# One-core graph and expert kernel: register loads grouped by batches, stores cut by 32 partitions, and half of a product on ScalarE

## The chip, the cores and the metric

The kernel runs as one program on 1 core of a Trainium2 chip. The metric is the device time of one launch in microseconds (us), the median of 3 runs. A profiled execution is a launch of its own; its span runs from the first to the last instruction of the program.

The engines are named as the profile does: PE is TensorE's matmul, PEld its weight load, DVE is VectorE, ACT is ScalarE, POOL is GpSimd, and SP is SyncE, which issues most DMAs. A letter q behind a name (SPq, PEldq, DVEq) marks an entry of that engine's sequencer, which waits, loads registers or issues DMAs.

## The reference

The input is 3125 nodes with 256 features, 50000 edges (src, dst, weight), and the weights of 16 experts. After a layer norm, three rounds of sparse times dense follow, each with an L2 normalisation of the rows, and the mean over the input and the rounds is added to x. Then come a second layer norm and a mixture of experts (2 of 16 for each node), with a layer norm behind it.

```python
def _spmm(vals, row, col, h, n_nodes):
    msgs = vals[:, None] * h[col]
    return jax.ops.segment_sum(msgs, row, num_segments=n_nodes, indices_are_sorted=True)
...
    for _ in range(LAYERS):            # 3
        h = _spmm(vals, row, col, h, n_nodes)
        h = _l2_normalize(h)
        acc = acc + h
    return acc / (LAYERS + 1)
...
    x = x + _L0_gnn_ref(_layernorm(x, axis=-1), edge_weight, src, dst)
    x = x + _L0_ffn_ref(_layernorm(x, axis=-1)[None], ...)[0]
```

The call gives `src` as `row` and `dst` as `col`, and the edges are sorted by `dst`.

## The kernel before

The kernel makes the sparse matrix dense once, and then does the three rounds as dense products. Its phases follow each other with a barrier between them: tables, build (0 to about 474 us of the profile together), rounds, route, experts, combine. The change is in the build phase, in one table it reads, and in the address from which the rounds load what it stored.

**The build phase.** The dense matrix has a row for each dst node and a column for each src node (3200 columns, as 20 groups HI of LO = 160). Six nodes (CW) make a window, so a window is M = 6 x 20 = 120 partitions by 160 columns. A step takes one tile of 128 edges, in the partitions, against one window: the matmul of a one-hot of (node in window, column group), weighted by the edge's value, with a one-hot of the column in its group gives the window's sum. The value is split into three bf16 parts, so each step has three matmuls. B = 12 steps make a batch, and there are NB = 76 batches; all 12 windows of a batch stand in four PSUM banks, three windows a bank.

For one batch b the engines do this:

- DVE: `key_hot` (128x1536, a comparison with `key_tab`), `lo_hot` (128x1920), and three products `key_w[k] = key_hot * part k` (function `weigh`, 128x1536 each). Then `carry` of batch b-2: the window in which batch b-3 ended may go on in batch b-2, and its sum is added to the first window (128x160). For this DVE needs a register with the place of that window, which `slot_of` loads at the start of each run.
- PE: waits until batch b-2 is out of PSUM, loads 12 registers with the PSUM places of the 12 steps (one TENSOR_LOAD of 12 words, line 513), opens the four banks with matmuls of 2 columns (line 518), waits for `hot_ready`, and issues 36 matmuls of 128x160 (line 523), with a register operation for each three.
- ACT: four copies PSUM to SBUF of 128x480 (`evacuate`, line 432) into `win`, a ring of RING = 4 batches. It waits for the stores of batch b-4, whose place it takes.
- SP: loads the number of the batch's first window (line 400), waits for `carried`, and stores 5 pieces of 24 partitions (line 406), one into each of 5 DRAM tensors `a_0` to `a_4`. Windows of consecutive batches overlap by design (the later store of a window is the full one), so each piece waits until the same piece of the batch before has landed.

The order of the work is written out by hand. `batches` writes four batches before a loop, four in the loop's body, and four behind it. The one-hots have two buffers, so DVE starts batch b only when PE has finished batch b-2.

**The rounds phase** loads, for each of 5 passes, blocks of 128 rows by 640 columns (2560 bytes a row) of the stored matrix (line 608), splits them in two parts on ACT and DVE, and multiplies. Each pass before has its own DRAM tensor, which is why the partitions of a window are ordered by pass in `key_tab` (five iotas of 48 elements, line 188).

## Time and profile before

| | us |
|---|---|
| runs | 1612.67, 1612.77, 1617.57; median 1612.77 |
| the profiled execution's own time | 1628.98 |
| its span | 1627.2 |
| build phase: first `key_hot` of DVE to first DMA of the rounds | 52.9 to 473.9 |

Over the span PE is busy 77% (1260.5 us), DVE 72%, ACT 45%, POOL 12%. These shares are means over phases with different limits; those of the build phase are among the rows below, in a table by stretch whose columns are the stretch, its length, then for PE, PEld, DVE, ACT and POOL the busy time with the number of instructions, then the granted TensorE clock as a share, the mean busy share of 16 DMA engines, and GB/s.

### The profile page before, as it was taken

To read this page: it belongs to the slowest core of one execution; us is meant where nothing else is said; L and a number is where in the kernel's file an instruction comes from. 1 tells how busy PE (TensorE), PEld (TensorE's weight loads), DVE (VectorE), ACT (ScalarE), POOL (GpSimd) and SP (SyncE) were. 2 spreads that over 40 slices of the span, in tenths; PEclk is the share of its full clock that TensorE was granted. 3 is DMA by queue.
4 is the path that set the end of the run, shared out by engine and by line. 5 is a ranking of instruction groups with operands and counts; after the bars stand their busy time and mean duration, and the time that the engine had idled before them with its cause. 6 is when DMAs were issued, how large, how long until landed. Compare 5 with 4: busy or idle time off the path is not lost. (4 is left out here: it accounts for less than half of the span.)

```text
span 1627.2 us, 30449 instructions
## 1 busy us (share of the span) xinstructions
PE 1260.5 (77%) x9152; PEld 1129.8 (69%) x9153; DVE 1173.7 (72%) x2074; ACT 730.1 (45%) x1401; POOL 196.1 (12%) x203
## 2 busy tenths in 40 slices
PE   4467667667738999999999999999574899999200
PEld 1456666666637888888888888888472899999200
DVE  8899999999927665765556756666555788988347
ACT  2333333333325555655554655555231666666102
POOL 1200000000000000000000000000250433332470
PEclk8798888888869999999999999999755899999655
DMA  2176677767677666666666656665140785344652
GB/s 94 48 177 173 173 179 180 179 173 182 178 213 217 186 186 185 184 174 186 183 186 178 194 168 185 185 184 181 45 157 30 233 277 184 101 111 94 194 162 72
DMA packets 229026, 267.32 MB, mean 164 GB/s; under 512 B 16061, under 2 KB 172356, under 8 KB 228960
## 3 DMA queue, kind: packets, MB, share of 16 engines
q1 hardware_dynamic: 205696, 234.01, 50.2%
q0 software_dynamic: 6624, 16.90, 3.8%
q10 hardware_dynamic: 16640, 15.73, 3.4%
q14 instruction: 50, 0.41, 0.1%
q8 instruction: 16, 0.26, 0.1%
HBM read 175.51 MB, written 91.07 MB: 164 GB/s over the span
## 5 line engine op out<-in xcount | busy, mean ns | idle before, releaser
L830 PE MATMUL ps_rows<-h_both,a_high 128*128 (+1 forms) x1875 | 506.6, 398 | 37.2 <-DVE a_low L710 31.9
L710 DVE TENSOR_TENSOR a_low<-a_raw,a_high 128x640 fp32r<-128x640 f32 x375 | 305.5, 823 | 236.2 <-ACT a_high L640 233.5
L640 ACT ACTIVATE a_high<-a_raw 128x640 fp32r<-128x640 f32 x375 | 274.4, 740 | 294.5 <-PE ps_rows L833 271.7
L830 PEld LDWEIGHTS ps_rows<-h_both,a_high 128*128 128x128 f32 x1875 | 330.8, 191 | 95.0 <-issue 32.3
L523 PE MATMUL ps_w<-lo_hot,key_w 128*128 128x160 bf16 x2736 | 257.6, 262 | 58.2 <-DVE key_w L459 57.6
L833 PEld LDWEIGHTS ps_rows<-h_both,a_low 128*128 128x128 f32 x1875 | 276.1, 191 | 32.9
L523 PEld LDWEIGHTS ps_w<-lo_hot,key_w 128*128 128x128 bf16 x2736 | 242.0, 111 | 64.4 <-issue 62.9
L833 PE MATMUL ps_rows<-h_both,a_low 128*128 (+1 forms) x1875 | 284.7, 283 | 0.0
L432 ACT ACTIVATE win<-ps_w 128x480 f32<-128x480 f32 x304 | 148.9, 576 | 261.1 <-DMA a<-win 156.0
L459 DVE TENSOR_TENSOR key_w<-key_hot,tab_marks 128x1536 bf16<-128x1536 bf16 x228 | 208.7, 949 | 0.0
L1318 POOL DMA_INDIRECT x_t<-tokens,r_token x80 | 92.6, 1157 | 141.5 <-PE ps_x L1445 128.7
L1390 DVE TENSOR_TENSOR w_low<-w_raw,w_high 128x1024 fp32r<-128x1024 f32 x80 | 94.4, 1220 | 20.7 <-ACT w_high L1332 14.0
L1332 ACT ACTIVATE w_high<-w_raw 128x1024 fp32r x80 | 80.4, 1052 | 60.9 <-PE ps_o L1477 47.8
L1460 PE MATMUL ps_h<-x_high,w_high 128*128 128x256 f32 x320 | 94.4, 295 | 0.0
L1460 PE MATMUL ps_h<-x_high,w_low 128*128 128x256 f32 x320 | 91.1, 285 | 0.0
L1460 PE MATMUL ps_h<-x_low,w_high 128*128 128x256 f32 x320 | 91.1, 285 | 0.0
L1477 PE MATMUL ps_o<-w_high,hid_high 128*128 128x256 f32 x320 | 90.0, 281 | 1.3 <-DVE hid_low L1405 1.3
L451 DVE TENSOR_TENSOR key_hot<-key_tab,tab_marks 128x1536 bf16<-128x1536 bf16 x76 | 72.7, 957 | 25.1 <-issue 17.4
L1477 PE MATMUL ps_o<-w_low,hid_high 128*128 128x256 f32 x320 | 90.0, 281 | 0.0
L1477 PE MATMUL ps_o<-w_high,hid_low 128*128 128x256 f32 x320 | 89.7, 280 | 0.0
L453 DVE TENSOR_TENSOR lo_hot<-lo_tab,tab_marks 128x1920 bf16<-128x1920 bf16 x76 | 87.4, 1150 | 0.0
L976 POOL MEMSET all_ones<- 128x800 f32 x1 | 0.8, 764 | 696.8 <-POOLq L537 696.8
(223 smaller groups left out, 1396.8 us busy)
## 6 DMA issues: line engine op xcount, KB each, us to landing
a_raw<-a SPq DMA_DIRECT2D x375, 320.0 KB, 3.1
a<-win SPq DMA_DIRECT2D x380, 180.0 KB
w_raw<-in_L_ffn_w SPq DMA_DIRECT2D x32, 512.0 KB
results_sorted<-y_t ACTq DMA_DIRECT2D x40, 256.0 KB
b_t<-in_L_ffn_b ACTq DMA_DIRECT2D x40, 128.0 KB
hf<-in_x SPq DMA_DIRECT2D x1, 3072.0 KB
x<-in_x SPq DMA_DIRECT2D x1, 3072.0 KB
tokens<-hf SPq DMA_DIRECT2D x4, 768.0 KB
```

What stands on the lines that cost most here:

```text
L432: ins = nc.scalar.activation(win[:, i, bank * WIDE:(bank + 1) * WIDE], ps_w[:, i % 2, bank * 512:bank * 512 + WIDE], ACT.Copy)
L453: v.tensor_tensor(lo_hot[:, u, :, :, :], tab.lo_tab[:].unsqueeze(1).broadcast_to([P, PAIRS, LO, 2]), mark(b, 1, LO), ALU.is_equal).then_in ...
L459: v.tensor_tensor(key_w[:, u, k, :, :, :], key_hot[:, u, :, :, :], mark(b, 2 + k, P), ALU.mult).then_inc(hot_ready, 1)
L523: ins = mm(ps_w[:, u, bass.DynSlice(places[j], LO)], key_w[:, u, k, j // 2, :, j % 2], lo_hot[:, u, j // 2, :, j % 2], start=False, stop=F ...
L640: a.activation(a_high[:, u, :], a_raw[:, u, :], ACT.Copy).then_inc(high_split, 1)
L710: v.tensor_tensor(a_low[:, u, :], a_raw[:, u, :], a_high[:, u, :].bitcast(F32), ALU.subtract).then_inc(low_split, 1)
L830: nc.tensor.matmul(ps[:, banks[w][r], :], a_high[:, u, r * P:(r + 1) * P], both, start=first, stop=False, skip_group_check=True)
L833: ins = nc.tensor.matmul(ps[:, banks[w][r], 0:D], a_low[:, u, r * P:(r + 1) * P], upper, start=False, stop=last, skip_group_check=True)
L1318: g.indirect_dma_start(out=x_t[:, t % 2, h, :], out_offset=None, in_=y_dram, in_offset=bass.IndirectOffsetOnAxis(ap=routes.token[:, t * HA ...
L1390: v.tensor_tensor(w_low[n][:, u, :], of_expert(w_raw[n], e), w_high[n][:, u, :].bitcast(F32), ALU.subtract).then_inc(w_low_ready[n], 1)
L1460: ins = mm(ps_h[:, u, f, :], w[0][:, u, at], x[:, u, k, :], start=(n == 0), stop=(n == 3 * KD - 1))
L1477: ins = mm(ps_o[:, u, half, :], h[:, u, f, tokens], w[1][:, u, at], start=(n == 0), stop=(n == 3 * KF - 1))
```

## The change

Four things change, all for the build phase.

1. **DVE's carry places.** `slots_of` loads the places of four batches in one register load at the head of the loop's body, where each batch had its own load. DVE's loop runs over 18 bodies of four batches, with four batches ahead of it.
2. **PE's places.** `multiply` loads 24 registers on even batches (two batches' places), and none on odd ones.
3. **Stores.** There is one DRAM tensor `a_rows` with all 120 partitions of a window in a row, and four stores of 32, 32, 32 and 24 partitions. `key_tab` is one iota in natural order, and the rounds load 2560 bytes out of each row of 12800. `zeros`, the source of the rows that no window covers, grows from 640 to 3200 columns, and five padding DMAs become one.
4. **Half of the third product on ScalarE.** DVE makes `key_w[2]` for 3 of 6 pairs of steps (128x768 in place of 128x1536). ACT makes the other 6 steps with one ACTIVATE of 128x128 each, with the weights as scale, after a copy of 12 weights into `third_b`. ACT does this for batch b ahead of the evacuation of batch b-1. DVE (before `key_hot`) and PE (before the matmuls) wait for it by `third_ready`.

```diff
-        zeros = sb("zeros", [P, s.GROUP * P])
+        zeros = sb("zeros", [P, s.HI * LO])
+        third_b = sb("third_b", [P, 2, B])
...
+        PARTS = [slice(p, min(p + 32, M)) for p in range(0, M, 32)]
...
-                for w in range(s.PASSES):
-                    part = slice(w * CW * s.HG, (w + 1) * CW * s.HG)
+                for n, part in enumerate(PARTS):
                     if late(b, 1):
-                        sp.wait_ge(stored[w], b * 16)
-                    sp.dma_start(a_dram[w][bass.DynSlice(base, B), :, :].rearrange("i p l -> p i l"),
-                                 win[part, i, :].rearrange("p (i l) -> p i l", l=LO)).then_inc(stored[w], 16)
+                        sp.wait_ge(stored[n], b * 16)
+                    sp.dma_start(a_dram[bass.DynSlice(base, B), part, :].rearrange("i p l -> p i l"),
+                                 win[part, i, :].rearrange("p (i l) -> p i l", l=LO)).then_inc(stored[n], 16)
...
+            def third(b, u):
+
+                if late(b, 2):
+                    act.wait_ge(multiplied, b - 1)
+                    act.wait_ge(third_ready, (b - 1) * BY_ACT)
+                nc.scalar.activation(third_b[:, u, :], tab.marks[:, 4, steps(b)], ACT.Copy).then_inc(third_read, 1)
+                act.wait_ge(third_read, b + 1)
+                act.wait_ge(key_ready, b + 1)
+                for j in range(2 * DVE_PAIRS, B):
+                    nc.scalar.activation(key_w[:, u, 2, j // 2, :, j % 2], key_hot[:, u, j // 2, :, j % 2], ACT.Copy,
+                                         scale=third_b[:, u, j:j + 1]).then_inc(third_ready, 1)
...
-            batches(act, evacuate)
+            def run(b, i):
+                third(b, i % 2)
+                if late(b, 1):
+                    evacuate(b - 1, (i - 1) % RING)
...
+                n = DVE_PAIRS if k == 2 else PAIRS
                 dve.wait_ge(key_ready, b + 1)
-                v.tensor_tensor(key_w[:, u, k, :, :, :], key_hot[:, u, :, :, :], mark(b, 2 + k, P),
+                v.tensor_tensor(key_w[:, u, k, 0:n, :, :], key_hot[:, u, 0:n, :, :], mark(b, 2 + k, P)[:, 0:n, :, :],
                                 ALU.mult).then_inc(hot_ready, 1)
...
+            with dve.Fori(1, NB // RING) as it:
+                slots = slots_of(it * RING - 2, RING)
+                for i in range(RING):
+                    run(it * RING + i, i, slots[i])
...
                 if late(b, 2):
                     pe.wait_ge(evacuated, b - 1)
-                _, places = nc.values_load_multi_w_load_instructions(
-                    tab.place[0:1, steps(b)], engines=[mybir.EngineType.PE], min_val=0,
+                if u == 0:
+                    both = slice(b * B, (b + 2) * B) if isinstance(b, int) else bass.DynSlice(b * B, 2 * B)
+                    places[:] = nc.values_load_multi_w_load_instructions(
+                        tab.place[0:1, both], engines=[mybir.EngineType.PE], min_val=0,
...
                 pe.wait_ge(hot_ready, (b + 1) * 4)
+                pe.wait_ge(third_ready, (b + 1) * BY_ACT)
```

**PE, from the end of one batch to the end of the next but one, in the loop.** `tab_place` is the table of places, `ps_w` the PSUM banks, "ISA" a register operation. Before, every batch has its load:

```order
L523 MATMUL ps_w<-lo_hot,key_w 128x160 x3
L513 ISA [waits evacuated]
L513 TENSOR_LOAD tab_place
L518 MATMUL ps_w<-none 128x2 x4
L520 ISA
L523 ISA [waits hot_ready_b]
```

Now the even batch (the first six rows) has a load, and the odd one (the last six) has none:

```order
L547 ISA [waits evacuated]
L547 TENSOR_LOAD tab_place
L552 MATMUL ps_w<-none 128x2 x4
L554 ISA
L555 REGISTER_ALU [waits hot_ready_b]
L558 ISA [waits third_ready]
...
L552 MATMUL ps_w<-none 128x2 [waits evacuated]
L552 MATMUL ps_w<-none 128x2 x3
L554 ISA
L555 REGISTER_ALU [waits hot_ready_b]
L558 ISA [waits third_ready]
L558 MATMUL ps_w<-lo_hot,key_w 128x160 x3
```

It is still one load instruction, of twice the words, and it keeps its place ahead of the even batch's matmuls.

**ACT, one batch in the loop.** `win` is the ring that the stores read, `third_b` the copied weights. Before, a batch is its evacuation alone:

```order
L426 REGISTER_ALU
L428 REGISTER_ALU [waits carried]
L430 REGISTER_ALU [waits stored_3,stored_4,stored_2,tabs,stored_1,stored_0]
L432 ACTIVATE win<-ps_w 128x480 [waits multiplied]
L432 ACTIVATE win<-ps_w 128x480 x3
```

Now seven small operations of the next batch stand ahead of it:

```order
L429 ACTIVATE third_b<-tab_marks 128x12
L430 REGISTER_ALU
L433 ACTIVATE key_w<-key_hot,third_b 128x128 [waits key_hot_ready,third_read]
L433 ACTIVATE key_w<-key_hot,third_b 128x128 x5
L438 REGISTER_ALU
L440 REGISTER_ALU [waits carried]
L444 ACTIVATE win<-ps_w 128x480 [waits stored_3,tabs,stored_2,multiplied,stored_1,stored_0]
L444 ACTIVATE win<-ps_w 128x480 x3
```

The evacuation of batch b-1 is queued behind the small operations of batch b, which wait for DVE's `key_hot` of batch b.

## Rows read from the trace of the kernel before

**Rows 1.** The page: the span, busy time, and busy share of the DMA engines in 40 slices

```profile
span 1627.2 us, 30449 instructions
PE 1260.5 (77%) x9152; PEld 1129.8 (69%) x9153; DVE 1173.7 (72%) x2074; ACT 730.1 (45%) x1401; POOL 196.1 (12%) x203
DMA  2176677767677666666666656665140785344652
```

**Rows 2.** Busy time of each engine in the batch stage and in what follows it

```profile
75.00:455.00 380.00, 262.21 (x2876) 244.76 (x2876) 355.84 (x504) 142.35 (x292) 0.00 (x0) 0.85 0.69 176
455.00:475.00 20.00, 0.00 (x0) 0.00 (x0) 0.81 (x2) 0.59 (x2) 0.31 (x1) 0.51 0.63 160
```

**Rows 3.** The page: groups of instructions, with one duration and the idle time before

```profile
L432 ACT ACTIVATE win<-ps_w 128x480 f32<-128x480 f32 x304 | 148.9, 576 | 261.1 <-DMA a<-win 156.0
L459 DVE TENSOR_TENSOR key_w<-key_hot,tab_marks 128x1536 bf16<-128x1536 bf16 x228 | 208.7, 949 | 0.0
L453 DVE TENSOR_TENSOR lo_hot<-lo_tab,tab_marks 128x1920 bf16<-128x1920 bf16 x76 | 87.4, 1150 | 0.0
```

**Rows 4.** Two lines of VectorE: durations, and the first and last start

```profile
L451 DVE TENSOR_TENSOR key_hot<-key_tab,tab_marks x76: 946/958/960, 52.9 to 444.0; 128x1536 bf16<-128x1536 bf16 x76
L479 DVE SCALAR_TENSOR_TENSOR win<-win,same_b x76: 372/376/385, 66.6 to 455.3; 128x160 f32<-128x160 f32 x76
```

**Rows 5.** Timeline from 370 to 383 us: start, length, and idle time before

```profile
371.87 2.75 PE L523 MATMUL ps_w<-lo_hot,key_w 128*128 128x160 bf16 x36 [0.17 <-DVE key_w L459]
375.69 0.24 PE L518 MATMUL ps_w<-none 128*128 128x2 bf16 x4 [1.07 <-issue]
376.85 4.33 PE L523 MATMUL ps_w<-lo_hot,key_w 128*128 128x160 bf16 x36 [0.93 <-DVE key_w L459]
376.92 0.96 DVE L451 TENSOR_TENSOR key_hot<-key_tab,tab_marks 128x1536 bf16<-128x1536 bf16 x1
377.79 1.15 DVE L453 TENSOR_TENSOR lo_hot<-lo_tab,tab_marks 128x1920 bf16<-128x1920 bf16 x1
378.86 1.82 DVE L459 TENSOR_TENSOR key_w<-key_hot,tab_marks 128x1536 bf16<-128x1536 bf16 x2
381.53 0.38 DVE L479 SCALAR_TENSOR_TENSOR win<-win,same_b 128x160 f32<-128x160 f32 x1
381.83 0.95 DVE L451 TENSOR_TENSOR key_hot<-key_tab,tab_marks 128x1536 bf16<-128x1536 bf16 x1
```

**Rows 6.** Register loads: all of L513, those before 74 us, one alone, and L469

```profile
L513 PEldq TENSOR_LOAD <-tab_place x76: 855/2286/3171, 52.9 to 445.0; - x76
L513 PEldq TENSOR_LOAD <-tab_place x5: 855/1054/1669, 52.9 to 73.5; - x5
L513 PEldq TENSOR_LOAD <-tab_place x1: 2338/2338/2338, 373.3 to 373.3; - x1
L469 DVEq TENSOR_LOAD <-tab_slot x76: 302/506/1407, 58.4 to 449.3; - x76
```

**Rows 7.** TensorE in two stretches, each of one batch, with the granted clock

```profile
252.85:256.00 3.15, 2.76 (x37) 1.00 0.71 180
257.79:262.05 4.26, 4.23 (x36) 0.62 0.71 176
```

**Rows 8.** The stores of line 406, and the first DMAs after them

```profile
L406 SPq DMA_DIRECT2D a<-win x380: 302/762/1682, 75.2 to 469.4; - x190
473.89 2.28 SPq L608 DMA_DIRECT2D a_raw<-a  x5
```

**Rows 9.** Timeline: two memsets of GpSimd; and groups of small operations on ScalarE

```profile
50.56 0.63 POOL L419 MEMSET zeros<- 128x640 f32 x1
51.13 1.70 POOL L420 MEMSET win<- 128x1920 f32 x1
...
L646 ACT ACTIVATE h_both<-hf 128x256 fp32r<-128x256 f32 x75 | 29.7, 401 | 18.8 <-DVEq L800 18.8
L1344 ACT ACTIVATE b_t<-r_b 128x4 f32 x34 | 6.6, 194 | 0.0
```

More of the change, by code:

```diff
@@ L185, in _ @@
             g.memset(ones[:], 1.0).then_inc(iotas, 1)
[L186 to L189 removed]
+            g.iota(tab.key_tab[:, 0:M, :], pattern=[[1, M], [0, 2]], base=0, channel_multiplier=0, **kw)
             g.memset(tab.key_tab[:, M:P, :], -2.0)
@@ L360, in phase_build @@
         same_read = sem("same_read")
+        third_read = sem("third_read")
+        third_ready = sem("third_ready")
         key_ready = sem("key_hot_ready")
@@ L366, in phase_build @@
         padded = sem("padded")
-        stored = [sem(f"stored_{w}") for w in range(s.PASSES)]
+        PARTS = [slice(p, min(p + 32, M)) for p in range(0, M, 32)]
+        stored = [sem(f"stored_{n}") for n in range(len(PARTS))]
         block = ctx.enter_context(nc.Block())
@@ L381, in batches @@
         def batches(eng, run):
-            for i in range(RING):
-                run(i, i)
-            with eng.Fori(1, NB // RING - 1) as it:
+            for b in range(2 * RING):
+                run(b, b % RING)
+            with eng.Fori(2, NB // RING - 1) as it:
                 for i in range(RING):
@@ L394, in _ @@
             sp.wait_ge(tabs, 3)
-            for w in range(s.PASSES):
-                rows = a_dram[w].rearrange("i (c n) l -> (i c) (n l)", c=CW)[first:s.CH * P, :]
-                sp.dma_start(rows, zeros[0:s.CH * P - first, :]).then_inc(padded, 16)
+            sp.dma_start(a_dram.rearrange("i (c n) l -> (i c) (n l)", c=CW)[first:s.CH * P, :],
+                         zeros[0:s.CH * P - first, :]).then_inc(padded, 16)
             def store(b, i):
@@ L426, in evacuate @@
                     act.wait_ge(carried, b - 2)
-                    for w in range(s.PASSES):
-                        act.wait_ge(stored[w], (b - 3) * 16)
+                    for done in stored:
+                        act.wait_ge(done, (b - 3) * 16)
                 act.wait_ge(tabs, 3)
@@ L434, in evacuate @@
                 ins.then_inc(evacuated, 1)
-            batches(act, evacuate)
+            def run(b, i):
+                third(b, i % 2)
+                if late(b, 1):
+                    evacuate(b - 1, (i - 1) % RING)
+            batches(act, run)
+            evacuate(NB - 1, (NB - 1) % RING)
         @block.vector
@@ L466, in same, with slots_of @@
                 v.tensor_copy(same_b[:, u:u + 1], tab.same[:, one(b)]).then_inc(same_read, 1)
-            def slot_of(b):
-                return dve.value_load(tab.slot[0:1, one(b)], min_val=0, max_val=(B - 1) * LO)
+            def slots_of(b, n):
+                at = slice(b, b + n) if isinstance(b, int) else bass.DynSlice(b, n)
+                _, values = nc.values_load_multi_w_load_instructions(
+                    tab.slot[0:1, at], engines=[mybir.EngineType.DVE], min_val=0, max_val=(B - 1) * LO,
+                    skip_runtime_bounds_check_because="a slot is LO times the minimum with B - 1 of a count")
+                return values
             def carry(b, i, slot):
@@ L480, in carry, with run @@
                                        win[:, i, start], ALU.mult, ALU.add).then_inc(carried, 1)
-            def run(b, i):
+            def run(b, i, slot):
                 u = i % 2
-                slot = slot_of(b - 2) if late(b, 2) else None
                 one_hots(b, u)
@@ L494, in _ @@
             dve.wait_ge(tabs, 3)
-            batches(dve, run)
+            slots = slots_of(0, 2)
+            for b in range(RING):
+                run(b, b, slots[b - 2] if b >= 2 else None)
+            with dve.Fori(1, NB // RING) as it:
+                slots = slots_of(it * RING - 2, RING)
+                for i in range(RING):
+                    run(it * RING + i, i, slots[i])
+            slots = slots_of(NB - 2, 2)
             for b in (NB - 2, NB - 1):
-                slot = slot_of(b)
                 same(b, b % 2)
-                carry(b, b % RING, slot)
+                carry(b, b % RING, slots[b - (NB - 2)])
         @block.tensor
@@ L507, in _ @@
                    start=True, stop=True, skip_group_check=True)
+            places = []
             def multiply(b, i):
@@ L1665, in program @@
     s = Sizes(x.shape[0], x.shape[1], src.shape[0], gate_w.shape[1], w1.shape[2])
-    a_dram = [nc.dram_tensor(f"a_{w}", [s.WALL, s.CW * s.HG, s.LO], F32, kind="Internal").ap()
-              for w in range(s.PASSES)]
+    a_dram = nc.dram_tensor("a_rows", [s.WALL, s.M, s.LO], F32, kind="Internal").ap()
     y_dram = nc.dram_tensor("tokens", [s.N, s.D], F32, kind="Internal").ap()
```

24 lines of the change are left out of this document (11 added, 13 removed).

## The prediction, written before the changed kernel ran

> **What bounds the kernel now.** I start with the page: the span is 1627.2 us and no engine is busy all through, so the answer has to come by phase [rows 1]. The table by stretch shows the phase that the change touches, 75 to 455 us: VectorE is busy 355.84 of 380 us, TensorE 262.21, ScalarE 142.35, and the DMA engines 0.69 of their time, a share that stays between 6 and 7 tenths in every slice of the phase [rows 1, 2]. VectorE's own two lines give the pace. `key_hot` starts at 52.9 us for batch 0 and at 444.0 for batch 75, so a batch takes (444.0 - 52.9) / 75 = 5.21 us [rows 4]. In the timeline one batch goes from 376.92 to 381.83 without idle time: 4.91 us [rows 5]. The other 0.30 us are the mean of what the register load of the carry place leaves uncovered (`tab_slot`, 302 to 1407 ns, [rows 6]). So VectorE sets the phase, and it is not alone.
>
> Two others are near. TensorE needs 2.75 us for its 36 matmuls where the granted clock is 1.00 (2.4 GHz), and 4.2 to 4.3 where the stretch's mean is 0.62, most of it at 1.2 GHz [rows 5, 7]; between two batches it has an idle stretch that the page puts down to "issue", which is its own register load: in the timeline matmuls end at 374.62, the load that began at 373.3 takes 2.34 us to 375.63, and the bank openers follow at 375.69 [rows 5, 6]. The stores are the other: ScalarE's evacuation waits 156.0 us for them in all [rows 3], the last carry starts at 455.3 and the last store is issued at 469.4, 14 us later, and the rounds' first DMA at 473.89 [rows 4, 8]. A store queue that ends that late had no room to catch up.
>
> **VectorE's part.** From 1536 to 1920 elements the operation grows from 949 to 1150 ns [rows 3], 0.523 ns an element. Half of `key_w[2]` is 768 elements less: 0.40 us off each batch, 4.91 to 4.51. Of the place loads one in four stays, with four words. Its price lies between nothing (covered as most of the one-word loads are) and four times the dearest, 5.6 us a load; I take about 0.45 us uncovered, near what the one-word median of 506 ns with some words more gives, so 0.11 a batch. VectorE alone would then run at 4.62 us a batch.
>
> **ScalarE's part.** Evacuations cost 148.9 / 76 = 1.96 us a batch [rows 3]. A 128x128 operation lies between 194 ns (128x4) and 401 ns (128x256) [rows 9]; I take 0.29. Six and the copy of 12 weights (0.19) are 1.9 us, at most 2.6. Sum 3.9, at most 4.6 us: it fits under 5 us, but just about under 4.62. The order also fits: `third(b)` can begin 0.96 us after `key_hot(b)` starts and is done at about 2.9; TensorE's batch b-1 begins at that same start (376.85 and 376.92) and ends 2.75 to 4.33 us later [rows 5]. So the evacuation queued behind `third` is late by nothing in most batches, and `third_ready` comes 1.5 us ahead of VectorE's last product, for which TensorE waits anyway. Cost: nothing; if the operations cost 0.40 each, 0.1 to 0.2 us a batch in the case where VectorE bounds.
>
> **TensorE's part, which decides.** The change halves the number of place loads but doubles the words of each. A load of 12 words took 1.05 us (median) before the stores begin, at 74 us, and 2.29 us over all 76, at most 3.17 [rows 6]. So it is paid by the word, and the more so the busier the DMAs are. The least load of 12 words took 0.855 and the least load of one word 0.302 us, though on another engine: about 0.05 a word and 0.25 fixed. A load of 24 is twice the 12 less one fixed part: 2 x 2.29 - 0.25 = 4.3 us under today's traffic, 2 x 1.05 - 0.25 = 1.9 us without stores; the outer ends are 1.5 and 6.3 us. The traffic falls, as four stores take the place of five and the same bytes go out in less queue time, so I go a fifth of the way from 4.3 to 1.9: 3.8 us.
>
> What covers it is the sequencer's lead: the load began 1.3 us before the last matmul ended [rows 5, 6]. That lead doesn't grow with the words. From the end of the load to the first matmul another 0.35 us pass (375.63, the openers' 0.24, and the step to the matmuls). Two batches then take: idle 3.8 - 1.3 + 0.35 = 2.85; 36 matmuls after that pause, at the lower clock for most of them, 4.25 (as 4.23 and 4.33 after pauses in rows 5 and 7); openers 0.3; 36 matmuls after a busy stretch, 2.75. Sum 10.15, or 5.08 us a batch, in general load + 6.35 for two. That is above VectorE's 4.62: the bound moves to TensorE, and nearly all of VectorE's saving turns into a wait before `key_hot` for `multiplied`. The gain of the phase is (5.21 - 5.08) x 75 = 10 us.
>
> The Trainium skill (Runtime: NRT & Kernel Launch, section Instruction fetch mechanics) has a rule that speaks against this edit: such a load costs about 200 ns a register, even in bulk. The trace has 191 ns a word in the median of the loads under traffic and 88 before it, so it agrees only with stores in flight. By the page 24 words would take 4.8 us, which as an estimate gives 11.15 us for two batches.
>
> **The stores.** The same bytes leave in four pieces. SP issued 380 stores between 75.2 and 469.4 us, one in 1.04 us, without catching up. If time goes by the piece (24 or 32 partitions alike) a batch's stores fall from 5.2 to 4.2 us; if by the bytes, they stay at 5.2. I take 4.2 to 4.5, as the share of 0.69 leaves DMA engines unused. Then the queue catches up within the phase, and the end gains: today 473.9 - 455.3 = 18.6 us from the last carry to the rounds. Afterwards three more issues of 1.04, the 4.5 us from the last issue to the rounds as now [rows 8], and about 0.9 for carry and base load: 8.5. Gain 10 us.
>
> The Trainium skill (DMA: Bandwidth & Descriptors, section Why a DMA increments its semaphore by 16 and not by 1) says that a DMA runs on the largest number of engines up to 16 that divides the outer sizes: 12 for 24 partitions, 16 for 32. The busy share of 0.69 fits under the 0.75 that 12 of 16 allow. By it the busiest engines would carry 8/10 of the rows, the 4.2 us above; without it the 5.2 of the rival below.
>
> **The start.** VectorE waits for the memset of `win`, which stands behind `zeros` (0.63 us for 640 columns, 1.70 for 1920, [rows 9]). At 0.83 ns a column 3200 columns cost 2.1 us more, and the whole phase begins that much later. The iotas of `key_tab` run long before it, and the padding moves the same bytes. The rounds read the same 2560-byte rows with another step; TensorE bounds there, and I cost that at nothing.
>
> **Sum**, against the profiled execution's own 1628.98: -10 (phase) -10 (end) +2 (start) = -18, so 1611. The runs' median lies 16 us below that execution; the same difference from 1612.8 gives 1594 us.
>
> **Rivals.**
> - The load is cheap. If 24 words take under 2.9 us, two batches of TensorE fall under 2 x 4.62, and VectorE bounds at 4.62. For it: five loads of 12 words took 1.05. Against: the median of all 76, most of them under traffic, is more than twice that. The time: (5.21 - 4.62) x 75 = 44, with end and start 52 us less: 1561.
> - The load is dear, and the kernel gets slower. The place is the pause of TensorE ahead of each even batch. It eats the other 8 us from 4.3 us a load on (two batches in 10.65); at 4.8 us it is 5.58 a batch, 27 us more in the phase, and with end and start 1632. For it: 2 x 2.29, and the dearest 12 words (3.17); against: fewer stores in flight. The page's 200 ns a register would put it here.
> - The stores keep their 5.2 us a batch, as bytes and rows are the same. Then ScalarE's evacuation holds everything to the old pace, and the end doesn't shrink: +2, 1615, or a few us less or more by how the load falls. For it: the 156 us that ScalarE waits for them.
>
> **Chances.** The forecast 0.50, cheap load 0.16, dear load 0.22, stores 0.12. The forecast's own range is 1578 to 1611, for loads of 3.4 to 4.3 us. I take 0.3% (5 us) as what a measurement of this kernel can tell from no change. Faster: 0.43 of the forecast's 0.50, and 0.16, together 0.59. Within 0.3%: 0.07 of the forecast and 0.07 of the stores, 0.14. Slower: 0.22 and 0.05, 0.27. For 8 in 10 the range reaches from the cheap load's 1562 to the dear load's 1632.
>
> **What would show it.** The loads of `tab_place` in the new trace: 38, with a median near 3.8 us. The wait of `key_hot` should be put to PE and no longer to issue; the even batches of TensorE slow, the odd ones at 2.75 us. `key_w` of 768 elements at about 547 ns. ScalarE busy near 3.9 us a batch, hardly waiting for stores. The last store within 5 us of the last carry. VectorE's first `key_hot` at about 55 us. I am wrong in the mechanism if VectorE stays without waits, or if ScalarE waits for `a_rows` as long as now; and in the size if the median load lies outside 3.4 to 4.3 us.

## The result, and the profile after

The changed kernel takes 1605.12 us (median of 6 runs, 1603.68 to 1606.47) against 1612.72 us for the kernel before beside it (6 runs, 1611.52 to 1618.16). The ratio is 0.9948, 95% interval 0.9934 to 0.9961: faster by half a per cent. The forecast was 1594 us (18 less), with a range of 1562 to 1632. The direction and the range hold; the gain is less than half of what was forecast.

The page of the changed kernel, the lines that answer to [rows 1], and its table by stretch, which answers to [rows 2]; the second columns are the time that a stretch lasts, then each engine's busy time, the mean granted clock, the DMA share and GB/s:

```profile
span 1604.1 us, 31106 instructions
PE 1259.8 (79%) x9152; PEld 1135.5 (71%) x9153; DVE 1137.9 (71%) x2074; ACT 875.4 (55%) x1933; POOL 209.8 (13%) x199
DMA  3187777677787666656666666666222587334373
```
```profile
75.00:455.00 380.00, 257.39 (x2881) 246.85 (x2880) 325.47 (x507) 279.80 (x794) 0.00 (x0) 0.83 0.75 180
```

VectorE lost work (355.84 to 325.47 us of 380), ScalarE doubled its own (142.35 to 279.80), and the DMA share rose from 0.69 to 0.75. The two profiled spans differ by 23 us, yet the medians by 7.6: the execution of before that was profiled ran long by 16 us, so the spans must not be subtracted. The phases up to the end of the rounds can be: from there to the end of the program the profile before takes 468.1 us and the changed one 450.8, and that is where the excess lies.

The lines of VectorE that answer to [rows 4], the register loads that answer to [rows 6], and the first transfer of the rounds, as in [rows 8] (a load's line gives least, median and longest ns, then first and last start):

```profile
L470 DVE TENSOR_TENSOR key_hot<-key_tab,tab_marks x76: 944/949/959, 55.1 to 443.4; 128x1536 bf16<-128x1536 bf16 x76
L504 DVE SCALAR_TENSOR_TENSOR win<-win,same_b x76: 371/376/385, 67.6 to 453.3; 128x160 f32<-128x160 f32 x76
```
```profile
L491 DVEq TENSOR_LOAD <-tab_slot x20: 782/2286/3541, 54.3 to 447.6; - x20
L547 PEldq TENSOR_LOAD <-tab_place x38: 1622/3310/4654, 54.3 to 440.3; - x38
```
```profile
465.27 0.85 SPq L643 DMA_DIRECT2D a_raw<-a_rows  x2
```

From these the 8.6 us by which the rounds start earlier (473.89 to 465.27) add up: the start is 2.2 later (52.9 to 55.1), the 75 batches take 388.3 in place of 391.1 (2.8 less, pace 5.18 after 5.21), the step from the last `key_hot` to the last carry 1.4 less, and from there to the rounds 12.0 in place of 18.6 us, 6.6 less. So the end gave most of what it should; the phase, which should have given 10 us, gave 3. At the end SyncE was still late: its last load of a base starts 3.1 us after the last carry has ended (453.7), and the last store is issued at 460.4.

```profile
L401 SPq TENSOR_LOAD <-tab_base x76: 467/728/1170, 74.3 to 456.8; - x76
```

What ate the phase stands in the timeline, from one batch (381.61) to the two after it. Start, length, what, and in brackets the idle time before it:

```profile
381.32 0.38 DVE L504 SCALAR_TENSOR_TENSOR win<-win,same_b 128x160 f32<-128x160 f32 x1
381.61 0.95 DVE L470 TENSOR_TENSOR key_hot<-key_tab,tab_marks 128x1536 bf16<-128x1536 bf16 x1
383.31 0.24 PE L552 MATMUL ps_w<-none 128*128 128x2 bf16 x4 [3.46 <-issue]
383.63 4.98 PE L558 MATMUL ps_w<-lo_hot,key_w 128*128 128x160 bf16 x36
385.82 0.38 DVE L504 SCALAR_TENSOR_TENSOR win<-win,same_b 128x160 f32<-128x160 f32 x1
388.55 3.19 PE L558 MATMUL ps_w<-lo_hot,key_w 128*128 128x160 bf16 x36
389.37 0.96 DVE L470 TENSOR_TENSOR key_hot<-key_tab,tab_marks 128x1536 bf16<-128x1536 bf16 x1 [3.18 <-PE ps_w L558]
```
```profile
L491 DVEq TENSOR_LOAD <-tab_slot x1: 2923/2923/2923, 386.1 to 386.1; - x1
```

One batch passes in 4.50 us (381.32 to 385.82), as VectorE alone would have it. Then VectorE stands still for 3.18 us. The view blames TensorE, whose matmuls ended at 388.61; but the four-word load that began at 386.1 ended only at 389.0, and `key_hot` starts 0.3 us behind that. The two limits end 0.4 us apart, and either alone would hold the batch. The new waits in the build phase (75 to 450 us, total, times, longest):

```profile
PE ps_w L552 <- issue: 90.9, 36, 4.2
ACT win L444 <- PE ps_w L558: 57.6, 23, 3.9
DVE key_hot L470 <- PE ps_w L558: 31.2, 14, 3.8
DVE key_hot L470 <- issue: 17.3, 7, 3.1
ACT win L444 <- DMA a_rows<-win: 12.9, 8, 4.4
```

The stores are out of the way (156.0 us of ScalarE's waiting became 12.9). `key_hot` now waits for both TensorE and its own load. Within each four batches, the first three pass at about 4.5 us and the one that ends in VectorE's load at 7.3 (means over batches 8 to 74, from the starts of `key_hot`: 4.51, 4.63, 4.50, 7.33).

### The profile page after: what moved, and what is told of

It is laid out like the page before. It is cut to its first block and busy times, and to the rows that moved or that the text cites. A ratio compares the mean times of both kernels' runs of the same rounds, so it can differ in the third digit from the quotient of the medians.

```text
span 1604.1 us, 31106 instructions
## 1 busy us (share of the span) xinstructions
PE 1259.8 (79%) x9152; PEld 1135.5 (71%) x9153; DVE 1137.9 (71%) x2074; ACT 875.4 (55%) x1933; POOL 209.8 (13%) x199
## 5 line engine op out<-in xcount | busy, mean ns | idle before, releaser
L479 DVE TENSOR_TENSOR key_w<-key_hot,tab_marks 128x1536 bf16<-128x1536 bf16 (+1 forms) x228 | 178.2, 814 | 0.0
L433 ACT ACTIVATE key_w<-key_hot,third_b 128x128 bf16<-128x128 bf16 x456 | 144.5, 426 | 38.2 <-DVE key_hot L470 36.9
L1353 POOL DMA_INDIRECT x_t<-tokens,r_token x80 | 104.4, 1305 | 131.5 <-PE ps_x L1480 118.7
L1425 DVE TENSOR_TENSOR w_low<-w_raw,w_high 128x1024 fp32r<-128x1024 f32 x80 | 94.4, 1220 | 17.6 <-ACT w_high L1367 12.9
L552 PE MATMUL ps_w<-none 128*128 128x2 bf16 x304 | 18.9, 166 | 91.3 <-issue 91.3
```

The source lines that it names most:

```text
L433: nc.scalar.activation(key_w[:, u, 2, j // 2, :, j % 2], key_hot[:, u, j // 2, :, j % 2], ACT.Copy, scale=third_b[:, u, j:j + 1]).then_inc ...
L479: v.tensor_tensor(key_w[:, u, k, 0:n, :, :], key_hot[:, u, 0:n, :, :], mark(b, 2 + k, P)[:, 0:n, :, :], ALU.mult).then_inc(hot_ready, 1)
L1353: g.indirect_dma_start(out=x_t[:, t % 2, h, :], out_offset=None, in_=y_dram, in_offset=bass.IndirectOffsetOnAxis(ap=routes.token[:, t * HA ...
L1425: v.tensor_tensor(w_low[n][:, u, :], of_expert(w_raw[n], e), w_high[n][:, u, :].bitcast(F32), ALU.subtract).then_inc(w_low_ready[n], 1)
```

## The experiments

The theory T: VectorE's four-word load, uncovered at the head of the loop body, and TensorE's pair of batches with its 24-word load are two limits nearly level. Taking away one runs into the other. The rivals: R1, VectorE's load is the only limit; R2, TensorE's load is, as the prediction had it. The times are medians of 5 to 12 executions beside the kernel before, unless said otherwise. Each kernel has one profile, and that one execution can lie some us off the median. What the profiles show of the phases:

| | pace, us a batch | first DMA of the rounds | rounds, first to last start of a matmul |
|---|---|---|---|
| before | 5.21 | 473.9 | 680.5 |
| changed | 5.18 | 465.3 | 683.3 |
| `a_covered` | 5.05 | 453.6 | 683.2 |
| `a_slots1` | 5.20 | 464.5 | 680.3 |
| `a_places12` | 5.25 | 469.7 | 680.1 |
| `a_both1` | 5.14 | 460.3 | 680.2 |
| `b_stores` | 5.43 | 482.7 | 680.2 |
| `b_half` | 5.28 | 478.8 | 681.3 |
| `c_cov12_row127` | 4.90 | 454.1 | 683.5 |
| `c_cov12` | 4.70 | 428.9 | 680.5 |
| `c_best` | 4.63 | 426.3 | 679.6 |

No edit touches the rounds; what the 3 us there are is told where the prediction is answered.

**VectorE's load covered (`a_covered`).** The same load, moved behind the second product of the body's first batch:

```diff
                 weigh(b, u, 1)
+                if load is not None:
+                    slots[:] = slots_of(load, RING)
...
-                slots = slots_of(it * RING - 2, RING)
```

> Changed kernel, but VectorE's load of four carry places stands behind the second weighed product of the body's first batch, where the sequencer would otherwise wait, and no longer at the loop head ahead of key_hot. Theory T (two limits nearly level: VectorE's four-word load at the loop head, 2.29 us in the median and 2.8 us of pause per four batches; TensorE's 24-word load): the pause ahead of key_hot goes, TensorE's load stays, a batch takes 5.0 to 5.1 us where it took 5.21, so 8 to 15 us less than the changed kernel, 1590 to 1597. Rival R1 (VectorE's load is the only limit, TensorE's pause is slack): 4.55 to 4.65 a batch, 1560 to 1566. Rival R2 (TensorE's load alone sets the pace, VectorE's load lies in its shadow): no change, 1605, and key_hot waits for PE by 2.8 us in four batches.

Measured 1592.16 us (1586.66 to 1595.88), ratio 0.9858 [0.9836, 0.988]: 13 us under the changed kernel, with nothing of the work removed. One such load and the operations on either side of it, and the waits of the phase:

```profile
L491 DVEq TENSOR_LOAD <-tab_slot x1: 3327/3327/3327, 358.0 to 358.0; - x1
```
```profile
358.54 1.82 DVE L479 TENSOR_TENSOR key_w<-key_hot,tab_marks 128x1536 bf16<-128x1536 bf16 x2
361.49 0.15 DVE L486 COPY same_b<-tab_same 128x1 f32 x1 [1.13 <-issue]
```
```profile
DVE key_hot L470 <- PE ps_w L564: 25.5, 20, 2.5
DVE same_b L486 <- issue: 10.2, 14, 1.5
```

The load takes 3.33 us, longer than where it stood, and yet costs 1.13, because two products were already queued when it began. What is left is TensorE (25.5 us in 20 waits). R1 (1560 to 1566) and R2 (1605) fall, T stands. The pace of 5.05 us is what the prediction had for TensorE alone (5.08).

**One-word loads on VectorE (`a_slots1`)**, each at the head of the batch that carries, instead of four words:

```diff
-                slots = slots_of(it * RING - 2, RING)
                 for i in range(RING):
-                    run(it * RING + i, i, slots[i])
+                    run(it * RING + i, i, slots_of(it * RING + i - 2, 1)[0])
```

> Changed kernel, but VectorE loads one carry place at the head of each batch, as before the change. T: each one-word load (0.5 us) leaves 0.2 to 0.3 us uncovered, VectorE alone would run at 4.8, TensorE's 24-word load holds the pace at 5.0 to 5.1: 1590 to 1599. R1: 4.75 to 4.85 a batch, 1575 to 1580. R2: 1605.

Measured 1601.31 us (1600.63 to 1602.83), 0.9923 [0.9906, 0.9941]: 4 us under the changed kernel, 2 above the upper end of T's range. But the build phase hardly moved. Its pace is 5.20 us where T had 5.0 to 5.1, the rounds start 0.8 us earlier than in the changed kernel, and 3.0 us of the difference between the two profiles lie in the rounds. TensorE fills this pace by itself: its load of 24 words takes 3.60 us here (mean of batches 8 to 71) and starts 0.69 us before the matmuls ahead of it end; with 0.37 us on to the next matmuls, 3.99 and 2.88 us for two batches of them and 0.30 between, a pair makes 10.5 us. T had the right limit and too low a price. The one-word load took 695 ns, not the 506 of before.

**Twelve words on TensorE (`a_places12`)**, loaded for every batch, VectorE's four-word load left:

```diff
-                if u == 0:
...
-                        tab.place[0:1, both], engines=[mybir.EngineType.PE], min_val=0,
+                    tab.place[0:1, steps(b)], engines=[mybir.EngineType.PE], min_val=0,
```

> Changed kernel, but TensorE loads 12 places for each batch, as before the change; VectorE's four-word load stays at the loop head. T: VectorE's 4 x 4.5 + 2.8 us for four batches stay, 5.2 a batch, so 1603 to 1606. R1: the same, 1605. R2 (TensorE's 24-word load alone): a pair of batches falls from 10.4 to about 9.9, and the time by 10 to 20 us, 1585 to 1595.

Measured 1606.59 us (1602.93 to 1608.64), 0.9952 [0.9934, 0.9969], the changed kernel's time within the scatter and half a us above T's range. With VectorE's load in the way TensorE's grouping doesn't show in the time. In the profiles the rounds start 4.4 us later than in the changed kernel and are 3.2 us shorter, so a small gain of the grouping is not excluded.

**Neither grouping (`a_both1`)** (both edits above; the stores and ScalarE's half product stay):

> Changed kernel without both groupings of loads: new stores and the half product on ScalarE alone. T: VectorE 4.8 a batch, TensorE with 12 words each near 4.9 to 5.0: 1585 to 1595, under each of the kernels that undo one grouping. R1: 4.8 a batch, 1575 to 1580, the same as with the single carry places alone. R2: as with the 12 places alone, 1585 to 1595.

Measured 1600.39 us (1598.41 to 1602.76), 0.9918 [0.99, 0.9935], 5 us under the changed kernel, but 5 above T's range. So the two grouped loads as they were placed cost more than they saved (in the profiles the rounds start 5.0 us earlier). T had the price of the ungrouped loads too low; `b_stores` shows why.

**The stores alone (`b_stores`)**, added to the kernel before (its a_rows buffer and four stores a batch, three of 32 partitions and one of 24; the text below says three):

> The kernel before with the changed a_rows buffer, iota and stores alone (three stores of whole rows by 32 partitions); the loads of places and VectorE's third product stay as before. Theory T (in the middle of the build phase VectorE's own chain and TensorE's pace, not the stores, set the pace): the pace stays within 0.05 of before's 5.215 us a batch, the tail from the last carry to the rounds' first a_raw transfer falls from 18.6 us to about 11, the start costs about 2 us; time 1604 to 1609 us, ratio about 0.996. Rival (the stores set before's pace: ScalarE waited 156 us for them): the pace falls by 0.1 us or more a batch as well, 1590 to 1600 us. Rival (the whole rows cost nothing and bring nothing): 1613 us.

Measured 1620.38 us (1615.0 to 1624.74, 11 runs), 1.0045 [1.003, 1.0059]: slower, against every theory. Its lines of VectorE, and waits in the phase:

```profile
L446 DVE TENSOR_TENSOR key_hot<-key_tab,tab_marks x76: 946/958/960, 54.3 to 461.4; 128x1536 bf16<-128x1536 bf16 x76
L464 DVEq TENSOR_LOAD <-tab_slot x76: 307/890/1097, 59.8 to 467.5; - x76
```
```profile
DVE key_hot L446 <- issue: 32.5, 62, 1.0
ACT win L427 <- DMA a_rows<-win: 9.5, 2, 4.9
```

The first of these waits in the kernel before, in the same stretch:

```profile
DVE key_hot L451 <- issue: 17.2, 37, 1.0
```

The stores no longer hold ScalarE, and the end is shorter (from the last `key_hot` to the rounds 21.3 us in place of 29.9). But the pace went from 5.21 to 5.43. In the kernel before, SyncE issued a batch's stores 6.4 us (mean) behind its carry; now they go out 0.16 us (median) behind it, upon VectorE's next load, whose median rises from 506 to 890 ns. VectorE has no slack there, so the 0.2 us a batch is paid in full: its waits for its own load grow by 15.3 us (17.2 to 32.5), and the 75 batches by 16. A faster store queue made another engine slower.

**Half the third product alone (`b_half`)**, the kernel before with that edit:

> The kernel before with half of the third product moved to ScalarE alone; stores and register loads as before. If VectorE's own work sets before's pace, it falls by up to the 0.40 us a batch that the half product takes, and the time would be 1583 to 1590 us. If the stores of before (about 5.2 us from issue to landing) or TensorE's pair of batches are level with VectorE, as T says, the pace falls by no more than 0.1 us a batch and the time is 1605 to 1613 us; a_both1 (both edits, 1600.4 us, pace 5.140) then holds about the sum of this and b_stores.

Measured 1616.09 us (1613.58 to 1625.29, 12 runs), 1.0023 [1.0008, 1.0039]: slightly slower, and above both ranges. (The 5.2 us in the text is the time in which a batch's stores leave; no run shows it as one store's way from issue to landing.)

```profile
ACT win L449 <- DMA a<-win: 62.0, 50, 3.7
ACT key_w L438 <- DVE key_hot L475: 30.2, 31, 1.6
DVE key_hot L475 <- issue: 25.2, 36, 1.6
DVE key_hot L475 <- ACT key_w L438: 23.5, 32, 1.7
```

With the old stores ScalarE's queue has an evacuation that waits for a store ahead of the next half product, and VectorE waits for ScalarE in turn (SyncE is 8.8 us behind the carries here, mean). Each part alone costs 3 to 7 us; both together (`a_both1`) gain 13. Neither could be priced alone; that they remove each other's bound is how I read it: without the old stores ScalarE's wait for them is 18.2 us in `a_both1` and not 62.0.

**What makes a load dear (`a_row127`).** The first idea, theory P, was the memory side of partition 0, which the first stores read too. Tables on all partitions, loads from row 127 (SyncE's is shown, the other two are changed alike):

```diff
-                base = sp.value_load(tab.base[0:1, one(b)], min_val=0, max_val=s.W - 1)
+                base = sp.value_load(tab.base[127:128, one(b)], min_val=0, max_val=s.W - 1)
```

> The changed kernel, with the tables of slots, places and bases worked out on all 128 partitions and the register loads of VectorE, TensorE and SyncE reading row 127 instead of row 0. Theory P (the loads are dear because the stores read the carried rows of the same partitions' side of the memory at the same moment; two of three stores touch the lower 64 partitions): VectorE's four-word load falls from 2.29 us to about 1.0 to 1.5, TensorE's 24 words from 3.31 to about 2.3 to 2.8, pace 4.8 to 5.0, 1575 to 1595 us. Rival (any store under way slows a load, whichever partition it reads): loads within 0.2 us of the changed kernel's, time 1603 to 1608 us. Rival (no relation to stores): the same, 1605 us; the two rivals are told apart by loads that start while no store is under way.

Measured 1605.08 us (1602.7 to 1606.74), 0.9945 [0.9929, 0.9961], no change. VectorE's loads take 2149 ns in the median, TensorE's 3706, SyncE's 1076 (2286, 3310 and 728 in the changed kernel): nothing gained, that idea is wrong.

**Thin stores (`a_thin`, `b_thin`).** Each store cut to one partition, so that its data is 1/24 to 1/32; the rest of the output rows is filled with zeros ahead of the first store, which lengthens the start. One profile each, read from 200 to 400 us only:

```diff
-                                 win[part, i, :]
+                                 win[part.start:part.start + 1, i, :]
```

> The changed kernel with each of its four stores a batch cut to one partition (the rest of the output rows is filled with zeros by transfers ahead of the first store, so the output differs and the start is longer; only the pace of the build phase is read). Theory S (VectorE's and TensorE's register loads are dear because store data moves at the same time): the four-word load falls from 2.29 us to about 1.0 and the 24-word load from 3.31 to about 1.65, as in the first batches, where no store is under way; the last batch of four falls from 7.33 to about 6.0 us and the pace from 5.18 to about 4.85 us a batch. Rival N (the loads are dear for a reason of their own, such as where they stand in the instruction stream): loads and pace within 5% of the changed kernel's.

> b_stores (the kernel before with the changed stores alone, pace 5.429, one-word load 0.89 us, twelve-word load 2.42) with each store cut to one partition, as in a_thin. Theory S: the one-word load falls to about 0.31 us, the twelve-word load to about 1.1, and since VectorE's chain sets the pace there, it falls by about the load's 0.58 us, to 4.85 to 4.95 us a batch. Rival N: pace within 0.1 us of 5.43. If the loads fall but the pace doesn't, VectorE's load was not on the path.

First the changed kernel with thin stores, then the `b_stores` kernel with them:

```profile
L492 DVEq TENSOR_LOAD <-tab_slot x10: 961/966/967, 208.4 to 392.1; - x10
L548 PEldq TENSOR_LOAD <-tab_place x20: 1717/1748/1757, 202.8 to 396.6; - x20
L407 SPq DMA_DIRECT2D a_rows<-win x157: 764/768/822, 200.6 to 399.3; - x157
L471 DVE TENSOR_TENSOR key_hot<-key_tab,tab_marks x40: 949/957/960, 199.1 to 397.9; 128x1536 bf16<-128x1536 bf16 x40
```
```profile
L465 DVEq TENSOR_LOAD <-tab_slot x39: 300/326/369, 202.5 to 396.6; - x39
L509 PEldq TENSOR_LOAD <-tab_place x39: 943/974/985, 202.4 to 396.2; - x39
L447 DVE TENSOR_TENSOR key_hot<-key_tab,tab_marks x39: 950/958/960, 203.3 to 397.4; 128x1536 bf16<-128x1536 bf16 x39
```

The DMA share in that stretch is 0.03. The four-word load falls from 2.29 to 0.97 us, 24 words from 3.31 to 1.75, one word from 0.89 to 0.33, 12 words from 2.42 to 0.97, and their spread all but vanishes. Store traffic in flight multiplies the price of a register load by 1.9 (24 words) to 2.7 (one word): theory S holds and N falls, on the loads. Bytes and packets fell together here, so which of the two it is stays open. On the pace it can't be read: both kernels run at 5.10 us a batch ((397.9 - 199.1) / 39; (397.4 - 203.3) / 38), because one-partition stores take SyncE 0.77 us each to issue. SyncE runs 12 us behind the carries and needs 5.0 us from the start of a base load to the end of the fourth issue, so it became the bound, and the expected 4.85 to 4.95 was missed.

**Both limits taken away (`c_cov12_row127`, `c_cov12`).** VectorE's load covered and 12 words on TensorE, reading row 127 and then row 0. The load stands behind the second product, as in `a_covered`; the first text says the first:

> The changed kernel with three edits: VectorE's four-word load moved behind the first product of the body's first batch (as in a_covered, 1592.2 us), twelve words of places per batch on TensorE (as in a_places12), and the register loads reading row 127 (as in a_row127). Theory T with P: pace 4.6 to 4.9 us a batch, 1560 to 1580 us. T alone (row 127 brings nothing): TensorE's pair with two loads of twelve words sets the pace at about 5.1 to 5.2, 1592 to 1600 us, no better than a_covered.

> c_cov12_row127 (1588.2 us, pace 4.897, held by the stores) with the register loads reading row 0 again, as the changed kernel does. SyncE's load of a base then takes about 0.8 us in place of 1.27. Theory: with both load costs out of the way, what is left is the last store's round trip (4.36 us from issue to landing, plus some 0.5 to the next issue), whichever row is read: pace 4.85 to 4.95, 1585 to 1592 us. If reading row 127 was what made the difference to a_covered, the pace goes back to 5.0 to 5.05 and the time to 1590 to 1596.

Row 127 took 1588.19 us (1587.72 to 1595.8), 0.9847 [0.983, 0.9865]. Row 0 took 1571.83 us (1566.57 to 1575.26), 0.9742 [0.9724, 0.9761], far below what was expected. T's own 5.1 to 5.2 us a batch for two loads of 12 words, and with it 1592 to 1600 us, was too slow for both.

With `c_cov12` the four combinations of the two loads are complete, and they are the proof of T:

| us | 24 words on TensorE | 12 words on TensorE |
|---|---|---|
| VectorE's load at the loop's head | 1605.12 (changed) | 1606.59 (`a_places12`) |
| VectorE's load covered | 1592.16 (`a_covered`) | 1571.83 (`c_cov12`) |

TensorE's 24 words cost 20 us once VectorE's load is covered, and nothing that shows while it isn't. The place of VectorE's load costs 13 us beside 24 words and 35 beside 12.

Why row 127 is the slower of the two shows in the trace. First row 127, then row 0, three views each: SyncE's base load, ScalarE's wait for the stores (75 to 420 us, and 75 to 405), and the row by engine of the same stretch:

```profile
L401 SPq TENSOR_LOAD <-tab_base x76: 478/1320/1411, 74.3 to 445.4; - x76
```
```profile
ACT win L444 <- DMA a_rows<-win: 68.6, 67, 2.2
```
```profile
75.00:420.00 345.00, 246.97 (x2788) 228.23 (x2786) 320.61 (x491) 273.50 (x764) 0.00 (x0) 0.87 0.80 186
```
```profile
L401 SPq TENSOR_LOAD <-tab_base x76: 463/890/1249, 74.2 to 420.5; - x76
```
```profile
ACT win L444 <- DMA a_rows<-win: 10.5, 11, 2.2
```
```profile
75.00:405.00 330.00, 222.96 (x2795) 205.37 (x2793) 318.50 (x490) 269.65 (x770) 0.00 (x0) 0.95 0.83 199
```

The pace is 4.90 against 4.70 us. My reason, the last store's own round trip of 4.9 us, is wrong, since the same stores with the same 2.7 to 4.4 us to landing went at 4.70. What differs is SyncE's base load, which stands between two batches' stores (1.32 against 0.89 us): SyncE is 9.3 us behind the carries with row 127 and 3.0 with row 0 (means), and ScalarE's wait follows it (68.6 against 10.5 us). The mean granted clock rose too, from 0.87 to 0.95. How the 0.2 us divides between the two I did not separate. The two profiled executions lie 29 us apart where the medians lie 16 apart, so these rows overstate the difference.

**The best version (`c_best`).** One-word loads on VectorE, each behind the second product of its batch; 12 words on TensorE, loaded before the wait for the evacuated buffer; `zeros` filled last, and only SyncE waits for it. The lines below are of the last two; VectorE's load stands behind the second product here too, not the first as the text says:

```diff
+            g.memset(win[:, RING - 1, :], 0.0).then_inc(tabs, 1)
             g.memset(zeros[:], 0.0).then_inc(tabs, 1)
-            g.memset(win[:, RING - 1, :], 0.0).then_inc(tabs, 1)
...
-            dve.wait_ge(tabs, 3)
+            dve.wait_ge(tabs, 2)
...
+                places[:] = nc.values_load_multi_w_load_instructions(
+                    tab.place[0:1, steps(b)], engines=[mybir.EngineType.PE], min_val=0,
...
                 if late(b, 2):
                     pe.wait_ge(evacuated, b - 1)
```

> The changed kernel with one-word place loads on VectorE, each behind the first product of its batch, twelve-word loads on TensorE moved ahead of the wait for the evacuated buffer, and the zeros for the end of the rows filled last, waited for by SyncE alone. VectorE's own work is about 4.5 us a batch plus at most 0.1 of load, TensorE's pair loses up to 0.7 us, the start loses the 2.2 us; the last store's round trip of 4.9 us is then the bound: pace 4.85 to 4.95, 1583 to 1590 us. If the loads don't stay covered, pace 5.05 to 5.15 and 1596 to 1604.

Measured 1561.47 us (1559.21 to 1567.9), 0.9679 [0.9656, 0.9702]: 44 us under the changed kernel, and 22 below the range's lower end, again because the stores' limit was set too high.

```profile
L470 DVE TENSOR_TENSOR key_hot<-key_tab,tab_marks x76: 949/956/960, 51.5 to 399.1; 128x1536 bf16<-128x1536 bf16 x76
L491 DVEq TENSOR_LOAD <-tab_slot x75: 300/672/1371, 60.8 to 403.3; - x75
```
```profile
ACT win L444 <- DMA a_rows<-win: 44.7, 63, 5.9
```

The pace is (399.1 - 51.5) / 75 = 4.63 us, the 4.51 of VectorE's own work and 0.12 more, and the start is 3.6 us earlier than in the changed kernel. ScalarE waits for the stores in 63 places, and SyncE, 7.4 us behind the carries (mean), takes 4.63 us from the start of a base load to the end of the fourth issue (median), as long as the pace. So SyncE has come level with VectorE, which itself waits only 6 us between 75 and 395 us. No run tells which of the two holds the pace.

## Why the prediction was right in direction and short in size

- **VectorE's part: the step that failed.** It priced what the four-word load leaves uncovered at about 0.45 us, "near what the one-word median of 506 ns with some words more gives". The pause is 3.18 us in the row at 389.37, and on average 7.33 - 4.5 = 2.8 us, 0.7 a batch where 0.11 stood. So VectorE's side came to 5.2 us a batch and not to 4.62, above the 5.08 of TensorE that was to decide. Two errors in one: the load takes 2.29 us, 570 ns a word under stores; and nothing covers it, as it follows the carry (0.38 us) with VectorE's queue empty. The prediction looked at the order of the loads on TensorE but not at where VectorE's lands. The upper end it kept, 5.6 us, did hold it. `a_covered` is the proof: placement alone gives 13 us, and the pace is then 5.05, TensorE's.
- **A misreading under it.** The prediction gave all of the 0.30 us a batch that VectorE stands idle in the kernel before to its register loads. In `b_thin`, where each of them takes 0.33 us, the pause ahead of `key_hot` is 0.49 us at the head of the loop's body and 0.00 to 0.04 in the other three batches (means, batches 12 to 71). The kernel before has 0.58 there and 0.06 to 0.16 elsewhere. A load that is free elsewhere is not free at the head, which adds 0.13 us even in `c_cov12`, where no load stands there. The sum moved all four words to that place and priced them by the mean of all places.
- **VectorE's saving** of 0.40 us a batch: right. Three batches in four pass in 4.50 to 4.63 us, against the 4.51 forecast.
- **TensorE's part.** The size was off, 3.31 us for 24 words where 3.8 was forecast, and the lead was 0.8 us, not 1.3: the load waits for the evacuation of two batches earlier, which ended only 0.1 us ahead of it. By the prediction's own sign (a median load outside 3.4 to 4.3 us) the size was wrong; that the two errors cancel is luck. After the pause the even batches took 4.09 us for their matmuls (mean), the odd 2.85, as expected, and a pair made about 10.4 us against 10.15. That TensorE would be a bound was right; that it would be the only one was not, and `key_hot` still waits for issue (17.3 us), which the prediction had excluded.
- **ScalarE's part.** A 128x128 operation takes 423 ns, not 290, but they start 0.30 us apart (six in 1.90 us in the timeline), so ScalarE is busy 3.8 us a batch (279.80 us in the 380 of the table) at no cost, as forecast (3.9).
- **The stores.** Right that they catch up: ScalarE's wait fell from 156.0 to 12.9 us, and the rival that kept their 5.2 us is out. The 4.2 us a batch was low: SyncE takes 4.63 us a batch for these stores in `c_best`. The Trainium skill (DMA: Bandwidth & Descriptors, section Why a DMA increments its semaphore by 16 and not by 1) allows 24 partitions 12 of 16 engines, a share of 0.75 at most. The traces agree, in that the five stores of 24 partitions stayed at 0.69 (0.68 in `b_half`) and the new ones reached 0.83, but no run here counts the engines. The end is 12.0 us for 8.5: 6.6 gained of 10. The sum put 0.9 us between the last carry and the stores for it; SyncE was 3.1 us late at that point, and the last store was issued 6.7 us after the last carry had ended, where "within 5" was the sign. What it did not see is the other edge: stores that follow at once fall upon the loads (`b_stores`).
- **The start**: 2.2 us later, as worked out (2.1).
- **The rounds** were put at nothing; from their first matmuls to their last they took 683.3 us in place of 680.5, 2.8 more. The changed kernel's line, its matmuls just before and after the first boundary of two layers, and its rows by engine there, with the granted clock third from the end:

```profile
L865 PE MATMUL ps_rows<-h_both,a_high x1875: 387/395/797, 470.0 to 1153.3; 128*128 x112, 128*128 128x512 f32 x76
```
```profile
699.74 1.32 PE L865 MATMUL ps_rows<-h_both,a_high 128*128 128x512 f32 x5
704.30 2.50 PE L865 MATMUL ps_rows<-h_both,a_high 128*128 128x512 f32 x5 [2.65 <-ACT halves L689]
```
```profile
697.00:703.00 6.00, 4.66 (x28) 3.92 (x26) 3.00 (x5) 2.96 (x6) 0.00 (x0) 1.00 0.68 181
703.00:707.00 4.00, 2.70 (x7) 2.22 (x8) 2.42 (x5) 1.86 (x4) 0.00 (x0) 0.57 0.28 81
707.00:711.00 4.00, 4.00 (x17) 3.47 (x16) 0.82 (x1) 0.87 (x2) 0.00 (x0) 0.57 0.34 92
```

  After TensorE's pause of 2.65 us between two layers the granted clock stood at 1.2 GHz for about 7 us, and five matmuls took 2.50 us where five had taken 1.32. The kernel before has a pause of like length there and kept 1.00 in that stretch. At the second boundary the clock falls in every kernel of the table, the one before included, so only the first makes the difference. It shows there in `a_covered` and `c_cov12_row127` too (and for a shorter time in `b_half`), and not in `a_slots1`, `a_places12`, `a_both1` or `c_cov12`; what decides it is open.
- **The rivals.** The cheap load did not come (3.31 is above 2.9), nor the dear one. The forecast's own range, for loads of 3.4 to 4.3 us, works out by its sums at 1579 to 1613 and not at 1578 to 1611; nothing hangs on it. The Trainium skill (Runtime: NRT & Kernel Launch, section Instruction fetch mechanics) gives about 200 ns a register; its figure comes from the registers that the runtime loads around a program, while the loads here read a table in SBUF. The measured price lies on both sides of it: 73 ns a word for TensorE's 24 and 242 for VectorE's four without store data, 138 and 570 with it.

Against the forecast of -10 for the phase, -10 for the end and +2 for the start stand -4.2 (pace and last batch), -6.6 and +2.2 up to the rounds, and +2.8 in them, or -5.8; the paired runs say -8. The rest of 2 us is within the scatter of the runs.

## What to carry to other kernels

Before grouping register loads, ask for each engine what is queued ahead of the grouped load: here a load of 3.3 us cost 1.1 behind two long operations, and a load at the loop's head its whole length. Price it from a load that runs beside the same transfers, since store traffic in flight made each load here 1.9 to 2.7 times as dear. And price edits that relieve different engines together: two that each made this kernel slower gained 0.8% as a pair.

## What the runs showed of the hardware

- A register load took, without the full stores (DMA share 0.03), 0.33 us for one word and 0.97 for four on VectorE, 0.97 for 12 and 1.75 for 24 on TensorE (medians); with them 0.89, 2.29, 2.42 and 3.31 in the same kernels. Spread over its words, and without the full stores, VectorE's load of four cost 242 ns a word, TensorE's of 24 73.
- Which row the load reads made no steady difference to VectorE's four-word load (2.29 us at row 0 and 2.15 at row 127; 2.51 and 2.87 in the other pair), but SyncE's one-word load went from 0.73 to 1.08 us with row 127, and from 0.89 to 1.32 in the other pair.
- A store of one partition took SyncE 0.77 us to issue, one of 24 or 32 partitions 0.60 in the median.
- VectorE paused 0.49 us ahead of `key_hot` where a load of 0.33 us stands at the head of the loop's body, 0.00 to 0.04 where the same load stands at the head of another batch (`b_thin`), and 0.13 at the loop's head with no load there (`c_cov12`).
